# The first dense layer inside the edge loop of a graph network: two blocks of 375 nodes in place of three blocks of 250

## What is computed

```python
msg = relu(layernorm(x)[src] + edge_attr @ W_e + b_e)      # per edge
h = (1 + eps) * layernorm(x) + segment_sum(msg, dst)       # per node, 1250 x 512
h = silu(batchnorm(h @ W1 + b1))                           # 1250 x 1024
h = silu(batchnorm(h @ W2 + b2))                           # 1250 x 512
x = x + h                                                  # then the experts
```

## Time and profile before

| what | value |
|---|---|
| runs | 602.73, 596.53, 601.85 us; median 601.85 |
| profiled execution | 596.02 us, span of its instructions 594.1 us |
| mean granted TensorE clock | 0.884 of full |
| busy over the span | PE 466.9 us (79%), DVE 394.3 (66%), ACT 318.8 (54%), POOL 254.8 (43%) |
| the loop's gathers on POOL | 167, the first at 32.3 us |

### The profile page before, as it was taken

The page is one execution under the profiler, slowest core; times in us unless marked ns, Lnnn a source line. Parts: engine busy times, 40 slices in busy tenths (PEclk is TensorE's granted clock), DMA queues, the critical chain, the costliest instruction groups (busy, mean ns, idle before and its releaser), DMA issues.

```text
span 594.1 us, 13290 instructions
## 1 busy us (share of the span) xinstructions
PE 466.9 (79%) x4679; PEld 313.1 (53%) x4679; DVE 394.3 (66%) x1012; ACT 318.8 (54%) x676; POOL 254.8 (43%) x245
## 2 busy tenths in 40 slices
PE   1557678987998898879999758203899999999990
PEld 1412222443443444224565346203799999999980
DVE  4955767777677777855797477675667676766430
ACT  2634655555566566655851194432166666666660
POOL 1067777777777777400000000000635556556331
PEclk9975957999899899989999968655699999999996
DMA  9759777777777777543764047700289999973331
GB/s 216 222 162 385 231 215 229 231 236 239 226 236 233 233 228 234 185 135 150 280 172 147 0 151 218 261 0 1 76 266 270 298 262 298 274 191 73 45 44 22
DMA packets 48982, 112.54 MB, mean 189 GB/s; under 512 B 7154, under 2 KB 7630, under 8 KB 48917
## 3 DMA queue, kind: packets, MB, share of 16 engines
q0 software_dynamic: 18992, 54.02, 33.1%
q1 hardware_dynamic: 29399, 57.16, 30.2%
q10 hardware_dynamic: 526, 0.51, 0.4%
HBM read 98.88 MB, written 12.79 MB: 188 GB/s over the span
## 4 chain that ended last, share of the span: by engine, by line
PE 63%; DVE 15%; ACT 7%; issue 6%; DMA 4%; POOL 2%; DVEq 2%; SPq 1%; POOLq 0%; ACTq 0%
PE bank L1367 23%; PE bank L1548 12%; PE bank L1358 7%; PE bank L1337 7%; DVE bank L984 4%; ACT big L616 3%; PE bank L1574 2%; PE bank L1529 2%; PE bank L1346 2%; PE bank L1411 2%; DMA xs_home<-in_x 2%; DVE rows_z L1187 1%; PE bank L1417 1%; PE bank L1538 1%; DMA big<-node_rows,edge_home 1%
## 5 line engine op out<-in xcount | busy, mean ns | idle before, releaser
L616 ACT ACTIVATE big<-bank 128x512 f32<-128x512 f32 x167 | 99.9, 598 | 79.8 <-DVE bank L984 75.8
L498 POOL DMA_INDIRECT big<-token_rows,idx x32 | 39.8, 1244 | 203.6 <-DVE idx L1241 195.2
L1367 PE MATMUL bank<-big,pair 128*128 128x156 f16 (+2 forms) x1056 | 106.5, 260 | 1.1 <-DVE big L1037 0.9
L488 POOL DMA_INDIRECT pair<-node_rows,edge_home x97 | 93.6, 965 | 29.5 <-issue 26.8
L1337 PE MATMUL bank<-big,edge_home 128*32 128x128 f32 x1336 | 73.9, 307 | 36.8 <-ACT big L616 36.4
L1367 PEld LDWEIGHTS bank<-big,pair 128*128 128x128 f16 x1056 | 80.9, 97 | 24.6 <-issue 1.4
L488 POOL DMA_INDIRECT big<-node_rows,edge_home x70 | 69.0, 986 | 51.2 <-issue 49.4
L1358 PE MATMUL bank<-edge_home 64*128 64x512 f16 x501 | 77.9, 421 | 3.2 <-DVE edge_home L957 3.2
L1337 PEld LDWEIGHTS bank<-big,edge_home 128*32 128x32 f32 x1336 | 28.8, 114 | 81.1 <-issue 55.0
L507 POOL DMA_INDIRECT out<-rows_z,idx x32 | 50.9, 1590 | 43.9 <-issue 25.0
L984 DVE TENSOR_TENSOR bank<-pair,bank 128x512 f32<-128x512 f32 x97 | 64.9, 689 | 6.0 <-PE bank L1358 4.6
(11 more groups left out here) (225 smaller groups left out, 769.4 us busy)
## 6 DMA issues: line engine op xcount, KB each, us to landing
raw<-in_L_ffn_w SPq DMA_DIRECT2D x12, 1024.0 KB, 9.4
edge_home<-in_L_ffn_w SPq DMA_DIRECT2D x6, 1024.0 KB, 9.3
pair<-in_L_ffn_w SPq DMA_DIRECT2D x6, 1024.0 KB, 9.8
edge_home<-in_edge_attr SPq DMA_DIRECT2D x19, 320.0 KB
xs_home<-in_x SPq DMA_DIRECT2D x10, 448.0 KB
xs_home<-in_L_ffn_w SPq DMA_DIRECT2D x4, 1024.0 KB, 8.5
aggT<-in_L_ffn_w SPq DMA_DIRECT2D x4, 1024.0 KB, 10.2
node_rows<-xs_home SPq DMA_DIRECT2D x5, 448.0 KB
```

Of the source, the lines that this page charges most:

```text
L488: pool.indirect_dma_start(row(t), None, node_rows, bass.IndirectOffsetOnAxis(src_i[:, t:t + 1], 0)).then_inc(row_in[t % RR], 16)
L498: pool.indirect_dma_start(xg[e % XR][:, a, :], None, token_rows, bass.IndirectOffsetOnAxis(idx[:, e, a:a + 1], 0)).then_inc(xg_in[e % XR], 16)
L616: act.activation(msg[:, t % MR, :], bank[t % PB][0:Q, :], ACT.Relu, scale=1.0 / E_SCALE).then_inc(msg_ready, 1)
L1367: last = pe.matmul(bk, weights(i, k), values(j, k), start=(begin and p == k == 0), stop=(end and p == 2 and k == n - 1), skip_group_check= ...
```

## The change

Two blocks of 375 nodes replace three of 250, so there are 16 products of 375 columns in place of 24 of 250. They stand at every second step: 20, 22, ... 34 and 37, 39, ... 51. The splits stand at steps 19 and 36, those of W1 at steps 13 to 16. `part16` needs 6000 bytes a lane in place of 4000, no longer fits behind W1 in `rows_z2`, and gets a buffer of its own. The last 500 nodes are treated as before.

```diff
-    ZC = 250
-    ZPARTS = 3
+    ZC = 375
+    ZPARTS = 2
     SLOPE, OFFSET = 21.5, 14.0
-    ZSTART = (13, 24, 36)
-    ZOFF = (0, 1, 2, 4, 5, 6, 8, 9)
+    ZSTART = (19, 36)
+    ZOFF = tuple(range(0, 16, 2))
     ZLAG = 1
...
-        part16 = rows_z2[:, HK * H2:HK * H2 + HK * ZC].bitcast(F16).rearrange("p (w k n) -> p w k n", w=2, k=HK)
+        part16 = sb("part16", [128, 2, HK, ZC], F16)
```

## The result

The changed kernel takes 603.61 us (median of 21 runs, 598.95 to 606.81); the kernel before, with 18 runs more than were shown above, 596.53 us (592.80 to 602.73). The ratio, estimated from all runs, is 1.0105, 95% interval 1.0079 to 1.0130 (the two medians alone would give 1.0119): about 6.3 us slower, where 4.7 were forecast. The first three runs of before had a median 5.3 us above that of all 21, so the forecast in absolute time (606.5) stands higher than the one in its difference.

What follows compares the result with a forecast made beforehand. PE's work bounds loop steps with a product, the chain from turn to next fold those without. Steps sum to 224.4 us; +0.5 gathers and -2.2 run-ahead give 222.7, +4.7, so 606.5 us against the median; range 598 to 613.

Steps and rivals of the forecast that it cites:

- within 1%: Outcome for the whole kernel's time: no change beyond about 1% (6 us); chance 0.52, against slower 0.38 and faster 0.10.
- The product: Twelve matmuls of 375 columns on PE in the loop: 2.03 us in place of 1.41, +0.62 each.
- Steps with a product: Loop steps 20-52 holding a product: PE full, 4.10 + 0.62 us (even) and 3.49 + 0.62 us (odd).
- Steps between: Loop steps between products: 2.79 + 0.14 us (odd) and 3.71 + 0.14 us (even), the statistics having grown.
- The longer copies: Node-column splits in steps 19 and 36: copy and subtraction of 1500 elements in place of 1000, +0.95 us each.
- The two corrections: Adjustments to the loop's step sum of 224.4 us: +0.5 for late gathers, -2.2 for engines running ahead.
- The run-ahead: Longer products let VectorE and ScalarE run ahead, shortening steps without a product: a quarter of 8.6 us taken, -2.2.
- The gathers: Plain steps 7-12 catch up with POOL's gathered rows near step 13: between 0 and 4.1 us, +0.5 taken.
- a sign of being wrong: Forecast wrong if VectorE waits for gathered rows in steps 10 to 13 by more than 1 us.
- B: Rival, chance 0.15: longer products fill the holes, steps between reach the tail's length, attributes cost nothing; -6.4 us, 595.5.
- C: Clock rival, chance 0.20: longer splits keep PE some 3.5 us more at half speed at each; +3.4, 610.0 us.
- D: Rival, chance 0.10: the removed split is worth more, holes and attributes were oversized by 3 us; +1.7, 603.5.

Runs made afterwards that it cites:

- e1_dense: The changed kernel with its 16 products at consecutive steps (20-27, 37-44) in place of every second step: 595.03 us, ratio 0.9959 to the kernel before.
- e2_late_stats: The changed kernel with the statistics of a product taken one step later, in the next step that holds a product: 598.05 us, ratio 1.0007 to the kernel before.

## Why the prediction was right

Right in direction and within its range: +6.3 us by the ratio, against +4.7. Of the outcomes "within 1%" had the best chance, 0.52; the measured 1.05% (0.79 to 1.30) lies on that border.

*What bounds the loop.* Held. PE's work sets a step with a product, the chain from the turn to the next fold one without; e1_dense and e2_late_stats moved that chain under a product in two different ways and won 8.7 and 5.8 us; in both it is the statistics that no longer lie bare.

*The product*, 2.03 us: measured 2.04. *Steps with a product*, 4.72 and 4.11: measured 4.74 and 4.12. *Steps between*, 2.93 and 3.85 before any correction: measured 2.92 and 3.85. *The longer copies*, +0.95 a split: 1.45 - 1.03 and 1.72 - 1.20 make 0.94. Step 19 took 5.94 (5.96 forecast), step 36 7.08 (6.52), with the clock at 0.91.

*The two corrections.* The run-ahead, -2.2 us, was wrong: it did not happen at all. The steps between products in the windows above are within a hundredth of what the uncorrected sum said, since the chain begins with the turn, and no length of the product hastens that. The gathers, +0.5, are not resolved: VectorE waited 2.2 and 1.0 us and steps 7-12 took 21.87 us against 18.5, but steps 13-18 gave some of it back (27.60 against 29.20). Steps 7-18 took 49.47 us here and 46.48 and 50.44 in e1_dense and e2_late_stats, whose code is the same that far; the forecast had 48.2. What I had named as a sign of being wrong, more than 1 us of such waits in steps 10 to 13, came in another place: 2.2 us already at step 9, 1.0 at step 12. Without corrections the sum had said +6.4. That this meets the +6.3 of the time is in part luck, as the next paragraph shows.

*This execution's extra.* The profiled pair differs by 10.5 us in the loop, not by 6.3. Against the uncorrected sum, steps 20-35 were 2.6 us longer than said, steps 7-12 3.4 longer and steps 13-18 1.6 shorter. In the former, the first product took 7.44 us at a clock of 0.60, where 4.72 + 1.84 was allowed for.

*B*, holes filled by the longer product: out, by the same rows. *C*, the clock: half of it. Around step 19 the low time is 2 x (0.08 x 5.94 + 0.40 x 7.44) = 6.9 us, as in steps 24 and 25 before (2 x 0.28 x 12.17 = 6.8); around step 36 it is 2 x (0.09 x 7.08 + 0.22 x 5.07) = 3.5. One of two splits fell on the far side, and so the named sign, a low clock lasting twice as long, came true for it. But step 19 was shorter than step 36, and in e2_late_stats, with the same splits, it was the other way round (3.4 us around step 19, 6.9 around step 36): the length of the split step does not decide it as I had put it. *D* is not separately tested; with the time at +6.3 nothing speaks for attributes and holes oversized by 3 us.

## What to carry to other kernels

Work that one engine has to do anyway is best placed where that engine would wait, and its place matters: the same matmuls in the same blocks were 1% slower at every second step and 0.4% faster at consecutive steps than the kernel before. Look not only at the work that is moved but at its small follower: here a statistics instruction of 0.54 us, harmless behind a product, became 0.45 us of most of the steps in which none stood. And work that fills early idle time may not be free to move later: with W1's split late, VectorE waited 1.3 to 3.8 us for gathered rows, though what that cost in time was not settled. Last, set profiles side by side only where the clock is the same in both, or look at many runs: around a split alone the clock made 2.8 us of difference between two executions.

## What the runs showed of the hardware that was not expected

PE's clock fell to its lower level not only after the splits. It also fell in the changed kernel's steps 31 and 32 (windows below), far from any split: step 31 holds an attribute split and no product, and PE was busy there for 3.09 of 4.62 us, with waits of 0.35 and 1.18 us. Such a step does not always bring it about: step 21 of the same execution, the last window, has the same two waits (0.35 and 1.18 us) and ran at a clock of 1.00.

```profile
169.92:174.54 4.62, 3.09 (x33) 0.93 (x31) 3.97 (x8) 2.94 (x7) 3.40 (x5) 0.78 0.84 258
174.54:179.83 5.29, 5.29 (x54) 2.30 (x50) 2.65 (x6) 1.80 (x4) 4.07 (x5) 0.87 0.76 223
129.66:133.63 3.97, 2.29 (x34) 0.83 (x32) 3.79 (x8) 2.78 (x7) 3.06 (x4) 1.00 0.78 226
```

With W1 early and all else alike, the loop of the profiled execution was 224.53 us in place of 228.49, of which only 2.6 us lie in steps 7-18: where the low stretches fall differs between executions. That this is why the 21 runs of the changed kernel spread over 7.9 us is likely, and was not shown; for it speaks that the seven shortest runs have a mean granted clock of 0.906 and the seven longest 0.890.
